# When the second weights of the first two expert tiles are sent, in an attention and mixture-of-experts block on one core

## The chip, the cores and the metric

The kernel runs on one core of a Trainium2 chip. The metric is the device time of one execution in microseconds. The kernel before took 765.93 us as the median of three runs, from 764.69 to 769.72. The profiled execution took 765.39 us, and the span of its instructions 763.7 us.

## The reference, cut to what matters

Two batches of 1024 tokens with 256 features go through causal self attention, cross attention over 77 encoder rows (each with 16 heads of 16), and a mixture of experts, each followed by a residual sum and a layer norm. The experts are what the change touches:

```
router_weights = softmax(x @ rw + rb)            # 8 experts
topw, topi = top_k(router_weights, 2); topw = softmax(topw)
h  = gelu(x @ w1[e] + b1[e])                     # 256 -> 1024
eo = h @ w2[e] + b2[e]                           # 1024 -> 256
out[t] = sum over the two chosen e of topw * eo
```

## The kernel before, in words

Each token is computed only for the two experts that it chose. The 4096 (token, expert) pairs are sorted by expert into at most 39 tiles of 128 rows (NSLOT); a tile has one expert. A tile gathers its 128 token rows from `tokens_scratch` (GpSimd, line 1899), turns them on TensorE (line 1050), multiplies by the first weights w1 (`half_up`, line 849, two halves of 16 matmuls), takes the gelu on ScalarE (line 1177), multiplies by the second weights w2 (`half_down`, line 855), scales on VectorE (lines 1402 and 1404) and puts the rows into `chosen_scratch` (GpSimd, line 1904). Both weights of a tile are 1 MB each. They are loaded into rings: three places for w1 (RING1), two for w2 (RING2).

The first nine tiles (NFIRST) hold tokens of batch 0 only and are worked in the midst of the attention of the last stages, which would otherwise leave TensorE waiting. For that, the string ORDER writes the order of all pieces of work by hand, a letter for a piece; `make_plan` turns it into one list, and every engine walks through that list and does its own part of each piece. So on each engine the order of the instructions is the order of the list, and a piece whose wait isn't over holds up all that the same engine has behind it.

The pieces that matter here:

- `t_weights` (letter B), four times, t = 0 to 3, on ScalarE (lines 1282 to 1291): loads w1 of tile t, from ScalarE's own DMA queue. Each load first reads the tile's expert into a register. From w1 of tile 4 on, line 1312 sends them behind a tile's gelus; from w2 of tile 2 on, line 1306 sends them ahead of them.
- `t_load` (A), on GpSimd: the gather of a tile's tokens.
- `t_turn`, `t_up`, `t_down`, `t_put` (N, U, Y, Z): the tile's work on TensorE, with the waits of lines 1048, 1056 and 1060 for the tokens, w1 and w2.
- `store` and `load` (s, l), on SyncE (lines 2070 and 2092): parts of projected queries go to memory and come back laid out by head.
- `max`, `gather`, `lay` and `score` (m or n, g or h, y, q): the maxima of the scores of a stage are taken (TensorE line 932, VectorE line 1472), split by GpSimd (lines 1974 to 1980), turned (TensorE line 943), sent to memory by SyncE (line 2100) and, when they have landed, back into the rows of the queries (line 2102). The scores (TensorE line 961) wait for that (line 955).

Between the second B and the fourth the list runs: second B, the bias load, one turn of x, the lists of rows, attention of stages 6 and 7, the gathers of tiles 0 to 5, turns of tiles 0 and 1, `t_up` of tile 0, stores and loads of stages 6 and 7, maxima of stage 6, turn of tile 2, third B, maxima, first half of `t_up` of tile 1, fourth B. Then come `t_down` of tile 0, `lay` of stage 6, the second half of `t_up` of tile 1, maxima of stage 7, the scores of stage 6, `t_up` of tile 2 and `t_down` of tile 1.

Of the kernel before, what the change touches and what calls it, by code (L numbers as in the profile page):

```python
# [57 lines left out]
RING1, RING2, RINGX, RINGY = 3, 2, 4, 3  # L58
# [314 lines left out]
def build(nc, x, ctx_in, par, wts, router_w, w1, b1, w2, b2, out):  # L373
# [3 lines left out]
    with stack:  # L377
# [782 lines left out]
        def scalar(act_e):  # L1160
# [8 lines left out]
            def weights2(j):  # L1169
                act_e.dma_start(w2_ring[j % RING2], w2_view[:, bass.ds(expert(j), 1)].rearrange("p e c n -> p (e c) n")).then_inc(  # L1170
                    weights2_in(j)[0], 16)
# [12 lines left out]
            for it in plan:  # L1184
                st = it.st
                bank = work[it.bank]

                if it.kind == "xt" and (it.t % 2 or not it.cross):
                    e.wait_ge(full[it.bank], it.use)
                    act_e.copy(xT[:, :, it.t * P:(it.t + 1) * P],  # L1190
                               bank[:, 0:D].rearrange("p (c n) -> p c n", c=KC)).then_inc(taken[it.bank], 1)

                elif it.kind == "proj":
                    key = st.n, it.at, it.g
                    n = int(st.cross) * 4 + it.at * KC + st.hh
                    bias = b_col[:, n:n + 1]
                    to = part_sb[ring_of[key] // NG][:, 0, it.t:it.t + it.w]
                    e.wait_ge(full[it.bank], it.use)
                    e.wait_ge(taken[columns.bank], columns.use)
                    e.wait_ge(parts_out[ring_of[key]], sent_before[key])  # L1200
                    if st.in_a_hurry:
                        act_e.activation(to, bank[:, 0:it.w], ACT.Identity, bias=bias).then_inc(first_part, 1)
                    else:
                        act_e.activation(to, bank[:, 0:it.w], ACT.Identity, bias=bias)
                        if it.n >= 2:
                            e.wait_ge(*third_ok(rest_after[it.n - 2]))
                        act_e.activation(f_sb[it.n % 2][:, 0:it.w], bank[:, 0:it.w], ACT.Identity,  # L1207
                                         bias=bias).then_inc(taken[it.bank], 1)

                elif it.kind == "rest" and st.in_a_hurry:  # L1210
                    key = st.n, it.at, it.g
                    z = projected[key]
                    e.wait_ge(taken[z.bank], z.use)
                    act_e.copy(part_sb[ring_of[key] // NG][:, 1, it.t:it.t + it.w],
                               f_sb[z.n % 2][:, 0:it.w]).then_inc(second_part, 1)

                elif it.kind == "v":
                    nk, rows = (1, SE) if st.cross else (4, P)
                    e.wait_ge(full[it.bank], it.use)
                    e.wait_ge(const_ok, 1)  # L1220
                    if st.n - 2 in pv_end and st.use > 1 and stage_cross[st.n - 2] == st.cross:
                        buf, use = prob_use(pv_end[st.n - 2], 1)
                        e.wait_ge(prob_taken[buf], use)
                    to = vac[st.slot][0:rows, :, 0:HD] if st.cross else va[st.slot][
                        :, it.t:it.t + nk, :, 0:HD].rearrange("p k h d -> p (k h) d")
                    act_e.copy(to, bank[0:rows, 0:nk * P].rearrange("p (k d) -> p k d", d=HD)).then_inc(taken[it.bank], 1)

                elif it.kind == "lay":
                    e.wait_ge(full[it.bank], it.use)
                    e.wait_ge(negm_out, 16 * it.n)  # L1230
                    act_e.copy(mT[0:3 * HH, :],
                               bank[0:3 * HH, 0:QG // 2].bitcast(bf16)).then_inc(taken[it.bank], 1)

                elif it.kind == "score":
                    rows = SE if st.cross else P
                    w = QG - (0 if st.cross else max(0, it.kb * P - it.g * QG))
                    pair, buf = it.n % 2, it.n % 4

                    e.wait_ge(pair_full[pair], it.n // 2 + 1)

                    if it.n == 2:
                        e.wait_ge(self_apart, 2)
                        e.wait_ge(cross_apart, 2)
                    act_e.activation(pt[buf][0:rows, :, 0:w], st2[pair][0:rows, :, 0:w], ACT.Exp,  # L1244
                                     scale=float(HD) ** -0.5).then_inc(pair_taken[pair], 1)

                elif it.kind == "normalise" and (it.g + it.quad) % 2:
                    buf, use = prob_use(weigh_last[it.n], 1)
                    e.wait_ge(prob_taken[buf], use)
                    if it.n >= 2:  # L1250
                        e.wait_ge(full[divides[it.n - 2].bank], divides[it.n - 2].use)
                    else:
                        e.wait_ge(full[columns.bank], columns.use)
                        for z in ctx_of:
                            e.wait_ge(full[z.bank], z.use)
                    act_e.copy(ot[it.n % 2], o_ps[:, :]).then_inc(o_taken, 1)

                elif it.kind in ("out_turn", "r_turn"):
                    e.wait_ge(full[it.bank], it.use)
                    if it.n >= 2:  # L1260
                        e.wait_ge(*turn_read(it))
                    act_e.copy((onT if it.kind == "out_turn" else rT)[it.n % 2],
                               bank[:, 0:D].rearrange("p (c n) -> p c n", c=KC)).then_inc(taken[it.bank], 1)

                elif it.kind == "out_apply" and it.b == 0:
                    t = it.b * TB + it.t
                    e.wait_ge(scaled, scaled_n[it.cross, it.b, it.t // QT])
                    act_e.activation(res[:, t, :], res[:, t, :], ACT.Identity, scale=rstd[:, t:t + 1],
                                     bias=shift[:, t:t + 1]).then_inc(centred, 1)

                elif it.kind == "w_exp":
                    tl = slice(it.b * TB, (it.b + 1) * TB)
                    e.wait_ge(exps_in, it.b + 1)
                    act_e.activation(ex_l[:, tl, :], lg[:, tl, :], ACT.Exp)
                    act_e.activation(pr[:, tl, :], pr[:, tl, :], ACT.Exp).then_inc(exps_ok, 1)

                elif it.kind == "w_diff":
                    tl = slice(it.b * TB, (it.b + 1) * TB)
                    e.wait_ge(diff_ok, it.b + 1)
                    act_e.activation(wgt[:, 1, tl], dw[:, tl], ACT.Exp).then_inc(second_ok, 1)  # L1280

                elif it.kind == "t_weights":

                    for p in range(2):
                        e.wait_ge(prob_taken[prob_use(last_self, p)[0]], prob_use(last_self, p)[1])
                    e.wait_ge(ej_ok, 1)
                    if it.t >= RING1:
                        e.wait_ge(*up_done(it.t - RING1))
                    weights1(it.t)
                    if it.t < RING2:  # L1290
                        weights2(it.t)

                elif it.kind == "t_turn":
                    e.wait_ge(full[it.bank], it.use)
                    if it.t == 0:
                        for z in find("out_tile", cross=False):
                            e.wait_ge(full[z.bank], z.use)
                    if it.t >= 2:
                        e.wait_ge(*up_done(it.t - 2))
                    act_e.copy(slot_xT[it.t % 2], bank[:, 0:D].rearrange("p (c n) -> p c n", c=KC)).then_inc(taken[it.bank], 1)  # L1300

                elif it.kind == "t_up":
                    if it.t >= 2:
                        e.wait_ge(*down_done(it.t - 2))
                    if it.at == 0 and it.t >= RING2:
                        weights2(it.t)
                    e.wait_ge(full[it.bank], it.use)
                    e.wait_ge(taken[b1_turned.bank], b1_turned.use)
                    half_gelu(it.t, it.at, bank).then_inc(taken[it.bank], 1)

                    if it.at == 1 and 0 < it.t < NFIRST - RING1:
                        weights1(it.t + RING1)
# [885 lines left out]
```

## Time and profile before

| | |
|---|---|
| median of 3 runs | 765.93 us (764.69 to 769.72) |
| profiled execution | 765.39 us, span 763.7 us |
| TensorE matmuls | 720.2 us busy, 94% of the span |
| VectorE, ScalarE, GpSimd | 498.4, 369.6, 286.6 us |
| mean granted TensorE clock | 0.972 of full speed |
| DMA | 140.29 MB, mean 184 GB/s |
| chain that ended last | PE 74%, issue 9%, DVE 7%, DMA 5%, POOL 3%, ACT 1% |

Engines in the rows: PE is TensorE's matmuls, PEld its weight loads, DVE VectorE, ACT ScalarE, POOL GpSimd, SP SyncE; a q behind the name is the engine's sequencer, where DMAs are issued. Times are in microseconds from the start of the span. DMA queues: q10 is the one that ScalarE issues to, q1 SyncE's, q0 GpSimd's.

### The profile page before, as it was taken

How to read it: one execution, taken by the hardware profiler on the slowest of the kernel's cores; microseconds unless marked ns; L12 is line 12 of the kernel's file. 1: busy time of each engine (PE TensorE's matmuls, PEld its weight loads, DVE VectorE, ACT ScalarE, POOL GpSimd, SP SyncE). 2: the span in 40 equal slices, each digit the busy share in tenths (PEclk: the TensorE clock that was granted, in tenths of full speed). 3: DMA queues.
4: the chain of work that ended last, by engine and by line, in shares of the span. 5: the costliest groups of instructions: out<-in, count | busy, mean ns of one | idle time of the engine just before them, and what ended most of it. 6: DMA issues, size and time to landing. Idle time of an engine off the chain costs nothing.

```text
span 763.7 us, 14561 instructions
## 1 busy us (share of the span) xinstructions
PE 720.2 (94%) x4969; PEld 483.5 (63%) x4969; DVE 498.4 (65%) x1376; ACT 369.6 (48%) x749; POOL 286.6 (38%) x558
## 2 busy tenths in 40 slices
PE   6889999999999999999998898999999999999984
PEld 4443434545464455555563676898999999999941
DVE  4679788688766877755766744365656666666436
ACT  3335466665657666677733355433323233332313
POOL 8305522543653553534733223212323322332114
PEclk9999999999999999999986998999999999999997
DMA  8964421243254022315017872686999999999755
GB/s 273 288 146 121 133 78 52 77 126 127 61 151 124 13 60 83 91 46 138 16 58 274 237 223 69 192 272 221 316 337 341 325 340 349 331 335 338 239 180 166
DMA packets 95154, 140.29 MB, mean 184 GB/s; under 512 B 11855, under 2 KB 81077, under 8 KB 92597
## 3 DMA queue, kind: packets, MB, share of 16 engines
q1 hardware_dynamic: 76357, 107.86, 44.8%
q10 hardware_dynamic: 15072, 22.02, 8.8%
q0 software_dynamic: 3648, 9.45, 3.5%
q8 instruction: 41, 0.67, 0.4%
q14 instruction: 36, 0.29, 0.1%
HBM read 110.65 MB, written 28.65 MB: 182 GB/s over the span
## 4 chain that ended last, share of the span: by engine, by line
PE 74%; issue 9%; DVE 7%; DMA 5%; POOL 3%; ACT 1%; DVEq 0%; SPq 0%; ACTq 0%; POOLq 0%
PE out_acc L984 12%; PE score_pair L961 10%; PE work L932 9%; PE score_pair L855 8%; PE work L849 7%; PE work L906 6%; PE work L1008 4%; PE score_pair L849 3%; DVE neg_part_max L1472 3%; PE work L855 3%; PE work L918 2%; PE work L992 2%; PE work L935 2%; DMA arena<-parts_scratch 1%; PE out_acc L849 1%
## 5 line engine op out<-in xcount | busy, mean ns | idle before, releaser
L1472 DVE TENSOR_REDUCE neg_part_max<-work 128x1 f32<-128x512 f32 (+4 forms) x368 | 213.3, 625 | 66.3 <-PE work L935 35.7
L1244 ACT ACTIVATE arena<-score_pair 128x1024 f32<-128x1024 f32 (+2 forms) x224 | 178.8, 839 | 76.6 <-PE score_pair L961 75.4
L932 PE MATMUL work<-arena 96*128 96x77 bf16 (+4 forms) x640 | 118.2, 277 | 10.1 <-ACT arena L1207 2.7
L961 PE MATMUL score_pair<-arena 99*128 99x512 bf16 (+2 forms) x448 | 105.8, 342 | 2.0 <-DMA arena<-negmax_scratch 1.6
L984 PE MATMUL out_acc<-arena 128*32 128x512 f32 (+4 forms) x896 | 104.6, 521 | 0.8 <-DVE arena L1492 0.8
L1904 POOL DMA_INDIRECT chosen_scratch<-arena,scatter_rows x36 | 35.4, 985 | 178.1 <-DVE arena L1404 177.1
L855 PE MATMUL score_pair<-arena 128*128 128x256 f32 x432 | 97.6, 379 | 0.0
L932 PEld LDWEIGHTS work<-arena 96*128 96x128 bf16 x640 | 49.2, 98 | 74.1 <-issue 30.2
L1960 POOL TENSOR_SCALAR_AFFINE_SELECT arena<-arena 128x256 f32<-128x256 f32 x128 | 51.5, 410 | 117.8 <-ACT arena L1244 116.6
L1177 ACT ACTIVATE arena<-work,expert_b_cols 128x128 f32<-128x128 f32 x180 | 51.1, 369 | 84.9 <-PE work L849 79.8
L849 PE MATMUL work<-arena 128*128 128x128 f32 x720 | 88.1, 280 | 0.3 <-issue 0.3
L849 PEld LDWEIGHTS work<-arena 128*128 128x128 f32 x720 | 85.7, 195 | 2.2 <-issue 1.3
L855 PEld LDWEIGHTS score_pair<-arena 128*128 128x128 f32 x432 | 80.1, 190 | 9.8
L1808 DVE STREAM_TRANSPOSE arena<-arena 32x64 f32<-32x64 f32 x304 | 71.6, 235 | 6.2 <-PE score_pair L849 2.1
L961 PEld LDWEIGHTS score_pair<-arena 99*128 99x128 bf16 (+1 forms) x448 | 38.2, 102 | 48.8 <-issue 21.9
L1402 DVE TENSOR_TENSOR arena<-score_pair,arena 128x256 f32<-128x256 f32 x27 | 11.5, 425 | 67.8 <-PE score_pair L855 58.9
L935 PE MATMUL work<-mask_qk,identb 128*128 128x128 bf16 x256 | 48.5, 219 | 0.0
L906 PE MATMUL work<-arena_more,arena 128*128 128x512 f32 x96 | 46.7, 615 | 0.1
L984 PEld LDWEIGHTS out_acc<-arena 128*32 128x32 f32 (+1 forms) x896 | 19.1, 108 | 34.8 <-issue 26.7
L1177 ACT ACTIVATE arena<-score_pair,expert_b_cols 128x128 f32<-128x128 f32 x72 | 20.5, 369 | 38.3 <-PE score_pair L849 37.3
L1008 PE MATMUL work<-arena 128*128 128x256 f32 x128 | 35.4, 411 | 0.6 <-ACT arena L1177 0.5
L849 PEld LDWEIGHTS score_pair<-arena 128*128 128x128 f32 x288 | 34.0, 194 | 0.4
(257 smaller groups left out, 962.5 us busy)
## 6 DMA issues: line engine op xcount, KB each, us to landing
arena<-in_L_xattn_e_w SPq DMA_DIRECT2D x54, 1024.0 KB, 6.2
arena<-parts_scratch SPq DMA_DIRECT2D x24, 768.0 KB, 5.8
arena<-in_L_xattn_e_w ACTq DMA_DIRECT2D x18, 1024.0 KB
parts_scratch<-arena_more SPq DMA_DIRECT2D x24, 384.0 KB, 2.6
parts_scratch<-arena_more SPq DMA_DIRECT2D x24, 256.0 KB, 3.0
parts_scratch<-arena_more SPq DMA_DIRECT2D x24, 128.0 KB, 2.9
residual<-in_x SPq DMA_DIRECT2D x4, 512.0 KB, 7.9
tokens_scratch<-residual SPq DMA_DIRECT2D x2, 1024.0 KB, 4.8
```

The lines of the kernel that those rows point to most:

```text
L849: m = pe.matmul(to[:, q * P:(q + 1) * P], w1_ring[j % RING1][:, c, f * P:(f + 1) * P], slot_xT[j % 2][:, c, :], start=(c == 0), stop=(c == ...
L855: m = pe.matmul(to, act[j % 2][:, c, :], w2_ring[j % RING2][:, c, :], start=(c == 0), stop=(c == FC - 1))
L906: m = pe.matmul(bank[:, 0:it.w], weights[:, c, st.hh * P:(st.hh + 1) * P], src, start=(c == 0), stop=(c == KC - 1))
L932: m = pe.matmul(bank[:, j * it.w:(j + 1) * it.w], qa[st.half(it.g)][0:R_S, h, n0:n0 + P], k, start=True, stop=not it.last)
L935: m = pe.matmul(bank[:, (j + 1) * it.w - P:(j + 1) * it.w], identb[:, :], mask_qk[:, :], start=False, stop=True)
L961: m = pe.matmul(st2[pair][0:rows, j, 0:w], k, qa[st.half(it.g)][0:R_M, h, skip:QG], start=True, stop=True)
L984: m = pe.matmul(o_ps[c * VW:(c + 1) * VW, skip:QG], v, pt[buf][0:rows, j, 0:QG - skip], start=first, stop=last)
L1008: m = pe.matmul(bank[:, 0:D], onT[o.n % 2][:, c, :], (w_cross if it.cross else w_self)[3][:, c, :], start=(c == 0), stop=(c == KC - 1))
L1177: m = act_e.activation(act[j % 2][:, c, :], bank[:, q * P:(q + 1) * P], ACT.Gelu, bias=b1_col[:, bass.ds(ex * FC + c, 1)])
L1244: act_e.activation(pt[buf][0:rows, :, 0:w], st2[pair][0:rows, :, 0:w], ACT.Exp, scale=float(HD) ** -0.5).then_inc(pair_taken[pair], 1)
L1472: dve.tensor_reduce(pm[:, it.at, it.t, it.h0:it.h0 + it.nh], bank[:, 0:it.nh * it.w].rearrange("p (j k) -> p j k", j=it.nh), AX.X, ALU.max ...
L1808: m = dve.transpose(to[b:b + SQUARE, :, a:a + SQUARE], of[a:a + SQUARE, :, b:b + SQUARE])
```

## The change

In the piece `t_weights` the condition and the tile of the second load change. Before, pieces 0 and 1 load w1 and w2 of their own tile. After, pieces 1 and 2 load w1 of their own tile and then w2 of the tile before. All other sends and all waits stay.

```
@@ -1287,8 +1287,9 @@
                     if it.t >= RING1:
                         e.wait_ge(*up_done(it.t - RING1))
                     weights1(it.t)
-                    if it.t < RING2:
-                        weights2(it.t)
+
+                    if 1 <= it.t <= RING2:
+                        weights2(it.t - 1)
 
                 elif it.kind == "t_turn":
                     e.wait_ge(full[it.bank], it.use)
```

The order in which ScalarE sends is then, by pieces (divided by bars): before, w1(0) w2(0) | w1(1) w2(1) | w1(2) | w1(3); after, w1(0) | w1(1) w2(0) | w1(2) w2(1) | w1(3).

## Rows read from the trace of the kernel before

**Rows 1.** The page: its first line, and TensorE's in its part 1.

```profile
span 763.7 us, 14561 instructions
...
PE 720.2 (94%) x4969; PEld 483.5 (63%) x4969; DVE 498.4 (65%) x1376; ACT 369.6 (48%) x749; POOL 286.6 (38%) x558
```

**Rows 2.** Timeline of ScalarE, 396 to 424: start, duration, engine, line, instruction, [idle before].

```profile
408.37 0.39 ACTq L1170 DMA_DIRECT2D arena<-in_L_xattn_e_w  x1
...
411.98 0.37 ACT L1190 COPY arena_more<-work 128x256 f32<-128x256 f32 x1 [2.81 <-PE work L872]
412.66 0.39 ACTq L1166 DMA_DIRECT2D arena<-in_L_xattn_e_w  x1
413.75 0.39 ACTq L1170 DMA_DIRECT2D arena<-in_L_xattn_e_w  x1
```

**Rows 3.** Timeline of ScalarE, 420 to 540.

```profile
433.39 0.39 ACTq L1166 DMA_DIRECT2D arena<-in_L_xattn_e_w  x1
439.36 1.14 ACT L1177 ACTIVATE arena<-work,expert_b_cols 128x128 f32<-128x128 f32 x4 [6.28 <-PE work L849]
440.38 0.39 ACTq L1166 DMA_DIRECT2D arena<-in_L_xattn_e_w  x1
...
446.65 0.39 ACTq L1166 DMA_DIRECT2D arena<-in_L_xattn_e_w  x1
```

**Rows 4.** Timeline of all engines, 436 to 482: TensorE's matmuls.

```profile
438.92 3.70 PE L855 MATMUL work<-arena 128*128 128x256 f32 x16
...
448.14 0.63 PE L961 MATMUL score_pair<-arena 99*77 99x512 bf16 x2
...
449.48 3.84 PE L849 MATMUL work<-arena 128*128 128x128 f32 x32
...
453.16 3.62 PE L855 MATMUL work<-arena 128*128 128x256 f32 x16
...
461.09 0.49 PE L943 MATMUL work<-identb,neg_max_parts 128*24 128x128 bf16 x4 [2.34 <-POOL neg_max_parts L1980]
```

**Rows 5.** DMA queues (packets, MB, share), 411.5 to 414.5, 417 to 421, 447.5 to 449.

```profile
q10 hardware_dynamic: 1021, 1.08, 106.9%
...
q10 hardware_dynamic: 1075, 1.13, 85.4%
q0 software_dynamic: 97, 0.30, 21.5%
...
q10 hardware_dynamic: 51, 0.21, 77.2%
```

**Rows 6.** Timeline of all engines, 402 to 436: the turn of tile 0.

```profile
422.10 0.44 PE L1050 MATMUL work<-ident,arena_more 128*128 128x128 f32 x2 [0.82 <-DVE arena L1458]
```

**Rows 7.** DMA queues, 433 to 437, 437 to 440.5, 444.5 to 445.

```profile
q1 hardware_dynamic: 90, 0.74, 71.5%
...
q10 hardware_dynamic: 259, 1.02, 85.2%
...
q1 hardware_dynamic: 32, 0.02, 13.8%
```

**Rows 8.** Timeline of SyncE's queue, 385 to 470: maxima out and back.

```profile
443.58 0.31 SPq L2100 DMA_DIRECT2D negmax_scratch<-arena_more  x1
445.64 0.24 SPq L2102 DMA_DIRECT2D arena<-negmax_scratch  x1
```

**Rows 9.** Chain of waits, 398.5 to 403: start, duration, what.

```profile
398.90 1.37 DMA negmax_scratch<-arena_more
...
400.29 2.20 DMA arena<-negmax_scratch
```

**Rows 10.** Timeline of GpSimd, 496 to 504: the put of a tile.

```profile
497.10 1.09 POOL L1904 DMA_INDIRECT chosen_scratch<-arena,scatter_rows  x1 [2.69 <-DVE arena L1404]
```

**Rows 11.** DMA queues, 497 to 500.5.

```profile
q10 hardware_dynamic: 968, 1.25, 101.7%
```

**Rows 12.** Stretches: us, busy per engine, granted clock, DMA share, GB/s.

```profile
462.00:468.00 6.00, 6.00 (x19) 4.47 (x20) 1.26 (x6) 3.41 (x4) 1.16 (x2) 0.50 0.20 52
```

More of the change, by code:

```diff
@@ L1289, in scalar @@
                     weights1(it.t)
-                    if it.t < RING2:
-                        weights2(it.t)
+                    if 1 <= it.t <= RING2:
+                        weights2(it.t - 1)
                 elif it.kind == "t_turn":
```

## The prediction

> **What bounds the kernel now.** I read the page first: TensorE is busy for 94% of the span [rows 1], so a late transfer costs time only where TensorE, which works in the written order, stands still for it; and once it does, hardly anything behind it gives the time back. Then I looked in the timeline of ScalarE for the sends that the change touches, in the table of DMA queues (q10 is ScalarE's queue, q1 SyncE's, q0 GpSimd's) for when their bytes move, and in the timeline of TensorE for who waits.
>
> The five DMA rows of the first sends are plain [rows 2]: w2 of tile 0 is sent at 408.37, w1 of tile 1 at 412.66, w2 of tile 1 at 413.75. w1 of tile 2 goes at 433.39 and w1 of tile 3 at 440.38 [rows 3]. The first users are far off: the second matmul of tile 0 starts at 438.92 and that of tile 1 at 453.16 [rows 4]. Neither weight is near its due time before the change.
>
> **The change, step by step.**
>
> *1. The first send loses w2(0).* ScalarE is free for one register load and one issue, 413.75 - 412.66 = 1.09 us [rows 2]. The next of its work on TensorE's way is the copy at 411.98, which waited 2.81 us for TensorE [rows 2]: gain 0. For the same reason w1(1) cannot be sent earlier than 412.66, as it stands behind that copy. So the queue, which moved four loads in one run before, now has a hole between w1(0) and w1(1).
>
> *2. The second send has w2(0) in place of w2(1).* Same count, same bytes. The queue moves 1.08 MB in 3.0 us [rows 5], that is 0.36 MB/us, so one load of 1.05 MB takes 2.9 us. Issue to first bytes is about 1 us, as w1(4), sent at 446.65, has only 51 packets moved by 449 [rows 5], so w1(1) and w2(0) need roughly 413.7 + 5.8 = 419.5 where the four in a row ended between 420 and 421 [rows 5]. w2(0) is due at 438.92: 19 us of cover. The token gathers (q0), which shared the last part of that run [rows 5], come 0.5 to 1 us earlier. Is that worth something? The turn of tile 0 at 422.10 waited for VectorE's line 1458, not for its gather [rows 6]. So 0; the bound for a gain is that whole wait, 0.82 us.
>
> *3. The third send gains w2(1).* It is issued at 433.39 + 1.09 = 434.5. ScalarE stood idle for 6.28 us before its next activation at 439.36 [rows 3], so its own 1.1 us cost nothing; if that cover were gone they would cost 1.1 us. w2(1) is due at 453.16. SyncE's load of 0.74 MB holds the engines till 437 [rows 7], w1(2) moves from 437 to 440.5 [rows 7], w2(1) then to 440.5 + 2.9 = 443.4: 9.8 us of cover. The load of q1 was issued before both and w2(1) stands behind w1(2) in its own queue, so it can't delay those two.
>
> *4. What stands behind w2(1).* w1(3), sent at 440.38, has to follow it: 443.4 + 2.9 = 446.3 in place of about 445. It is for a tile that comes after the second matmul of tile 1 at 453.16 [rows 4], so this alone is harmless. But SyncE sends the maxima of stage 6 out at 443.58 and, once they have landed, back in at 445.64 [rows 8]; the scores at 448.14 need them [rows 4]. In a quiet stretch the same pair took 1.37 and 2.20 us [rows 9]. Here the store took 2.06 us, and its 32 packets moved in 444.5 to 445, when w1(3) was ending [rows 7]: it already waits for what is ahead of it. That such waits are the rule here, the put of line 1904 shows: issued at 497.10, it has not one packet moved by 500.5, while q10 moved 968 from 497 on, alone in that table [rows 10, 11].
>
> So the store lands 1.3 us later. The load before had 448.14 - 445.64 - 2.20 = 0.3 us of room. TensorE then starts the scores 1.0 us late; the maxima that stand between these scores and the matmul at 449.48 keep their order, so there is no further room that I count on. From 449.48 TensorE works without a gap through 453.16; its next idle stretch ends at 461.09 by GpSimd's line 1980 [rows 4], which had itself waited for the put behind tile 1's second matmul: that shifts too. Between 0 (the 24 KB get in among the weights, as some of q0's packets did in the same stretch as q10's [rows 5]) and 3.6 us (second rival), and with the 0.82 us of step 2 as the bound of a gain, I take **+1.0 us**, the value that the store's own row is nearest to.
>
> A rule of the Trainium skill speaks against step 4. It says in "DMA: Bandwidth & Descriptors", section "Queues, rings and completion order", that each DMA engine goes round the queues that have work, packet by packet; by that rule SyncE's 24 KB would slip in between the weights and the sum would be 0 instead of 1.0 us, which is the rival "nothing moves" below. The put at 497.10 [rows 10, 11], which waited for the whole of another queue's backlog, doesn't agree with it.
>
> **Sum.** 0 + 0 + 0 + 1.0 = +1.0 us on the profiled execution of 765.39 us (span 763.7 [rows 1] and 1.7 around it): 766.4. The median of the three runs, 765.93, stands 0.54 above that execution, so the forecast is **766.9 us**.
>
> **The rivals.**
>
> *Second burst.* The return of the maxima would be sent at 445.64 + 1.3 = 446.9, and w1(4) is sent at 446.65 [rows 3]: the order of the two is turned round, which before it was not (445.64 against 446.65). If the load has to wait for w1(4)'s 2.9 us beside its own delay, it lands near 451.7 and TensorE stands still for 3.6 us. Such a gap has a second price: after the 2.34 us without work before 461.09 [rows 4], the granted clock was 0.50 (the lower level, 1.2 GHz) for the six microseconds from 462 [rows 12]. If the clock falls behind the new gap as well, the 7 us of matmuls at 449.48 and 453.16 [rows 4] lose about 6 / 2 = 3 us. This is the case that ends slower: 3.6 to 6.6 us, around 770.5. The point from which it decides is a store that lands after about 446.6. For it: the put at 497.10 [rows 10], and the tie above. Against it: a load's first packets trickle (51 in the 1.5 us from 447.5 [rows 5]), so that a small transfer may get in before them. It passes 1% (7.7 us) only if the clock stays low longer than in that stretch, or if the next gap gets longer too.
>
> *Nothing moves.* The queues mix well enough for 24 KB, as 97 packets of q0 and 1075 of q10 moved in one stretch of 4 us [rows 5], or the hole in step 1 lets everything drain sooner. The time is 765.9, the median of before. For it: w1(3) started slowly before, and it will start at once behind w2(1), so the end of the queue moves by less than I reckon.
>
> *Relief.* The calmer queue between 411.5 and 421 helps: the gathers are early, the wait of 0.82 us at 422.10 [rows 6] goes, and the later work falls so that part of the 6 us at half clock [rows 12] is won back, at most 3 us. Then 0.8 to 3.8 us faster, around 764. Against it: that wait was VectorE's, and the clock has no tie to these loads.
>
> *A weight that comes late.* w2(1) would have to take 18 us from its issue; the three loads sent from 408.37 on were all through by 421, in under 13 [rows 2, 5]. Chance nearly 0.
>
> **How the numbers follow.** Forecast 0.42, second burst 0.26, nothing moves 0.17, relief 0.15. A measurement of this kernel can tell about 1%, 7.7 us, from no change. Of the cases only the far end of the second burst (0.06) goes over that on the slow side, with 0.01 for what I haven't seen; on the fast side the relief case would need twice its bound: 0.03. That leaves 0.90 within 1%. The range: the relief case's middle less a little, 763.3, to the second burst with most of its clock loss, 771.5. It leaves out about 0.1 on each side. The runs of before spread from 764.69 to 769.72, so the ends are not wider than the scatter of single runs makes them.
>
> **What would show it.** Right, in the profile of after: on q10 w1(0), then a hole, then the 4 KB packets of w1(1) (259 for 1.02 MB [rows 7]) and only after 416 the 1 KB packets of w2(0) (1021 for 1.08 MB [rows 5]); w2(1) issued near 434.5 on ScalarE and moved between 440.5 and 443.5; the store of the maxima at 443.6 followed by its return at 446.5 to 447 rather than 445.64; a new short wait of TensorE's line 961 for that return, about 1 us; every later stage of TensorE as much later. Wrong: the return still sent within 2.1 us of the store and the scores at 448.1 (nothing moves); the scores at 451 or later with a granted clock of 0.50 behind them (second burst); the turn of tile 0 before 422.10 (relief). The forecast would be wrong altogether if ScalarE's third send came at another time, as when the maxima of stage 6 shift against it.

## The result, and the profile after

The kernel after took 771.12 us as the median of 20 runs (767.62 to 774.63), the kernel before 764.89 us as the median of 20 runs on the same chip (760.85 to 769.72). The ratio is 1.0082, with a 95% interval of 1.0065 to 1.0099: slower by 6.2 us. That is inside the range of 763.3 to 771.5 and within 1%, but it is not the forecast of 766.9; it is the rival called the second burst. The profiled execution took 772.72 us, 7.33 more than the one before.

The page's first lines, of after [rows 1]:

```profile
span 771.0 us, 14561 instructions
...
PE 722.3 (94%) x4969; PEld 485.4 (63%) x4969; DVE 498.7 (65%) x1376; ACT 369.7 (48%) x749; POOL 286.4 (37%) x558
```

TensorE is busy for only 2.1 us more, in a span that is 7.3 us longer: most of the time went into a wait.

The sends in the timeline of ScalarE, 404 to 450 [rows 2, 3]:

```profile
407.58 0.40 ACTq L1166 DMA_DIRECT2D arena<-in_L_xattn_e_w  x1
413.00 0.40 ACTq L1166 DMA_DIRECT2D arena<-in_L_xattn_e_w  x1
414.11 0.39 ACTq L1170 DMA_DIRECT2D arena<-in_L_xattn_e_w  x1
433.92 0.39 ACTq L1166 DMA_DIRECT2D arena<-in_L_xattn_e_w  x1
435.02 0.39 ACTq L1170 DMA_DIRECT2D arena<-in_L_xattn_e_w  x1
440.89 0.39 ACTq L1166 DMA_DIRECT2D arena<-in_L_xattn_e_w  x1
447.16 0.39 ACTq L1166 DMA_DIRECT2D arena<-in_L_xattn_e_w  x1
```

w1(0) is sent alone, w1(1) and w2(0) together at 413 to 414, w1(2) and w2(1) at 434 to 435, w1(3) and w1(4) behind them. Against the rows of before the sends from 413 on stand 0.3 to 0.5 us later; w1(0), which the change leaves alone, is 0.33 us later already (407.58 against 407.25). The turn of tile 0 was 0.39 us later too, and waited as it did before [rows 6]; timeline of TensorE, 420 to 425:

```profile
422.49 0.44 PE L1050 MATMUL work<-ident,arena_more 128*128 128x128 f32 x2 [0.81 <-DVE arena L1459]
```

So the first two parts of the change cost and gave nothing. Now SyncE's queue, 440 to 460: the maxima of stage 6 go out and, once they have landed, back in [rows 8].

```profile
444.09 0.31 SPq L2101 DMA_DIRECT2D negmax_scratch<-arena_more  x1
448.54 0.24 SPq L2103 DMA_DIRECT2D arena<-negmax_scratch  x1
```

The store took 4.45 us (448.54 - 444.09) where it took 2.06 before. Its return was then issued 1.38 us behind w1(4), where before it went 1.01 us ahead of it. The DMA queues show what each waited for: four stretches, 440.7 to 443.75, 443.75 to 446.25, 446.25 to 448, and 448 to 451.2.

```profile
q10 hardware_dynamic: 958, 1.06, 104.2%
...
q10 hardware_dynamic: 346, 1.00, 106.0%
...
q10 hardware_dynamic: 55, 0.16, 23.3%
q0 software_dynamic: 46, 0.13, 20.3%
q1 hardware_dynamic: 36, 0.02, 4.4%
...
q10 hardware_dynamic: 220, 0.90, 93.0%
```

First come the 1 KB packets of w2(1), then the 4 KB packets of w1(3), and only when that one had but 0.16 MB left did SyncE's (q1) and GpSimd's (q0) packets move at all. In the fourth stretch w1(4) has the engines; the return is issued at 448.54, and by 451.2 none of its packets has moved, while q10 moved 0.90 MB. TensorE, 445 to 470 [rows 4]:

```profile
453.20 1.07 PE L961 MATMUL score_pair<-arena 99*77 99x512 bf16 x2 [4.55 <-DMA arena<-negmax_scratch]
...
455.71 5.04 PE L849 MATMUL work<-arena 128*128 128x128 f32 x32
460.59 3.62 PE L855 MATMUL work<-arena 128*128 128x256 f32 x16
468.52 0.60 PE L943 MATMUL work<-identb,neg_max_parts 128*24 128x128 bf16 x4 [2.34 <-POOL neg_max_parts L1981]
```

The new wait is 4.55 us, and the 32 matmuls of line 849 took 5.04 us in place of 3.84. The granted clock says why; columns are the stretch, each engine's busy time and number of instructions, the clock, the share of the DMA engines and GB/s:

```profile
450.00:452.00 2.00, 0.00 (x0) 0.00 (x0) 0.00 (x0) 0.00 (x0) 1.43 (x7) 0.86 0.81 328
452.00:454.00 2.00, 0.80 (x2) 0.36 (x3) 0.00 (x0) 0.00 (x0) 0.42 (x3) 0.50 0.00 0
454.00:456.00 2.00, 2.00 (x16) 1.42 (x15) 0.79 (x2) 1.59 (x2) 0.00 (x0) 0.50 0.00 0
456.00:458.00 2.00, 2.00 (x11) 2.00 (x11) 1.93 (x6) 0.45 (x1) 0.00 (x0) 0.50 0.36 73
```

During the wait the clock falls from full speed (2.4 GHz) to half (1.2 GHz) and stays there to 458. Before, the whole stretch from 448 to 461 had it at full speed:

```profile
448.00:461.00 13.00, 10.75 (x85) 8.64 (x81) 7.20 (x20) 7.70 (x15) 5.02 (x20) 1.00 0.75 250
```

Behind 460.59 everything stands 7.4 us later, the wait at line 943 is the same 2.34 us, and nothing is given back up to the end.

**A measure for the experiments.** Single executions of one kernel scatter over 7 to 9 us, and the profiled ones differ in where the clock falls ahead of the place in question too: from 386 to 394 it was 0.57 before and after, but 1.00 in those of experiments 4, 5 and 6, though the change and these edits touch only what comes later. So absolute times of two executions are not compared. Besides the medians I use a stretch inside one execution: from the issue of the store of the maxima to the first matmul of tile 1's second product (line 855). It is 453.16 - 443.58 = 9.58 us before and 460.59 - 444.09 = 16.50 after: 6.92 us of the 7.33 lie in it.

### The profile page after: what moved, and what is told of

It is laid out like the page before. It is cut to its first block, busy times and chain, and to the rows that moved or that the text cites. A ratio compares the mean times of both kernels' runs of the same rounds, so it can differ in the third digit from the quotient of the medians.

```text
span 771.0 us, 14561 instructions
## 1 busy us (share of the span) xinstructions
PE 722.3 (94%) x4969; PEld 485.4 (63%) x4969; DVE 498.7 (65%) x1376; ACT 369.7 (48%) x749; POOL 286.4 (37%) x558
## 3 DMA queue, kind: packets, MB, share of 16 engines
q0 software_dynamic: 3648, 9.45, 3.4%
## 4 chain that ended last, share of the span: by engine, by line
PE 74%; issue 9%; DVE 7%; DMA 5%; POOL 3%; ACT 1%; SPq 0%; DVEq 0%; ACTq 0%; POOLq 0%
PE out_acc L984 12%; PE score_pair L961 10%; PE work L932 9%; PE score_pair L855 8%; PE work L849 7%; PE work L906 6%; PE work L1008 4%; DVE neg_part_max L1473 3%; PE score_pair L849 3%; PE work L855 3%; PE work L918 2%; PE work L992 2%; PE work L935 2%; DMA arena<-parts_scratch 1%; PE out_acc L849 1%
## 5 line engine op out<-in xcount | busy, mean ns | idle before, releaser
L961 PE MATMUL score_pair<-arena 99*128 99x512 bf16 (+2 forms) x448 | 106.6, 344 | 6.6 <-DMA arena<-negmax_scratch 6.0
L961 PEld LDWEIGHTS score_pair<-arena 99*128 99x128 bf16 (+1 forms) x448 | 38.4, 103 | 53.3 <-issue 21.9
```

What stands on the lines that cost most here:

```text
L961: m = pe.matmul(st2[pair][0:rows, j, 0:w], k, qa[st.half(it.g)][0:R_M, h, skip:QG], start=True, stop=True)
```

## The experiments

The theory: the cost is two delays in a row, the store behind w2(1) and w1(3) and the return behind w1(4), plus the clock that falls in the gap. The rivals: the later w2(0) costs something too; only one of the two delays decides; the clock doesn't matter.

**1. Only w2(0) moves; w2(1) stays where it was.**

```
-                    if it.t < RING2:
-                        weights2(it.t)
+                    if it.t == 1:
+                        weights2(0)
+                        weights2(1)
```

> Of the change only the move of w2(0) is done: second send w1(1), w2(0), w2(1); third send w1(2) alone. Theory 'backlog' (w2(1) ahead of w1(3) makes SyncE's 24 KB of maxima wait out and back): nothing stands in the queue at 443 that did not before, the store of the maxima takes about 2.1 us, TensorE's line 961 has no long wait at 448, time as before, within 0.2%. Rival 'first sends' (the hole after w1(0) and the later w2(0) cost the time): 5 to 7 us slower.

Measured 766.67 us against 764.5, ratio 1.0036 (1.0006 to 1.0067). The stretch is as before, 9.45 us; the store takes 1.94 and TensorE doesn't wait for its return:

```profile
447.76 0.31 SPq L2101 DMA_DIRECT2D negmax_scratch<-arena_more  x1
449.70 0.24 SPq L2103 DMA_DIRECT2D arena<-negmax_scratch  x1
...
457.21 3.62 PE L855 MATMUL work<-arena 128*128 128x256 f32 x16
```

But the whole was not as before, which was a miss: from the second send to the store this execution takes 33.69 us (414.07 to 447.76), where before took 30.92 (412.66 to 443.58), 2.8 us less. Three loads in one run from 414.07 on keep the queue full for longer, and now the turn of tile 0 does wait for its gather (timeline of TensorE, 410 to 432). The queues of 416.5 to 421 and of 421 to 424 stand below it. The clock was lower as well, 0.88 from 420 to 434 where before had 1.00:

```profile
424.22 0.41 PE L1050 MATMUL work<-ident,arena_more 128*128 128x128 f32 x2 [1.62 <-DMA arena_more<-tokens_scratch,gather_rows]
...
q10 hardware_dynamic: 1083, 1.69, 102.0%
...
q10 hardware_dynamic: 779, 0.78, 81.5%
q0 software_dynamic: 97, 0.27, 26.5%
```

That run of three exists neither before nor after, so this loss isn't one of the change. But the experiment alone doesn't acquit the later w2(0), as its interval lies above 1; for that the next one is needed. What it does show is a small transfer, the gather, that is late behind a run of loads.

**2. Only w2(1) moves.**

```
-                    if it.t < RING2:
-                        weights2(it.t)
+                    if it.t in (0, 2):
+                        weights2(it.t // 2)
```

> Of the change only the move of w2(1) is done: first send w1(0), w2(0); second send w1(1) alone; third send w1(2), w2(1). Theory 'backlog': all of the loss is here, store of the maxima 4 to 4.5 us, wait of line 961 near 4.5 us, 5.5 to 7 us slower than before. Rival 'first sends': as before, within 0.2%.

Measured 769.94 us, ratio 1.0077 (1.0045 to 1.0109): as slow as the whole change. The store takes 3.26 us (446.59 to 449.85), w1(4) is issued at 449.66, again ahead of the return, and TensorE waits. Store and wait are shorter than the 4 to 4.5 and 4.5 us expected:

```profile
452.99 1.07 PE L961 MATMUL score_pair<-arena 99*77 99x512 bf16 x2 [1.82 <-DMA arena<-negmax_scratch]
...
455.49 5.34 PE L849 MATMUL work<-arena 128*128 128x128 f32 x32
460.67 3.62 PE L855 MATMUL work<-arena 128*128 128x256 f32 x16
```

The stretch is 14.08 us, 4.5 more than before, of 5.4 in the profiled execution. Its store was also issued 3.0 us later than before (446.59 against 443.58), with the clock at 0.55 from 438 to 442 where before had 1.00; whether that belongs to the edit or to the execution isn't shown. So the later w2(1) alone makes this loss, with half the store's delay and under half the wait; the clock falls here too. Adding the later w2(0) to it, which is the whole change, costs nothing more that the medians show (1.0082 against 1.0077).

**3. The change, with w1(3) out of the store's way** (sent behind tile 1's gelus, ahead of w1(4)).

```
-                    weights1(it.t)
+                    if it.t < RING1:
+                        weights1(it.t)
...
+                    if it.at == 1 and it.t == 1:
+                        weights1(RING1)
```

> The changed kernel, but w1(3) is sent with w1(4) behind the second gelus of tile 1 (about 447) and not in the fourth send at 440.9. Theory 'backlog': the queue is empty from 443.8 on, the maxima go out in about 1.4 us and are sent back at 445.5, ahead of both loads; no long wait at 448 and the whole loss gone, 5 to 7 us faster than the changed kernel, the same as before or up to 0.7 us better. Rival 'ScalarE's issue' (the 1.1 us that w2(1) adds on ScalarE in the third send is what shifts the work): loss stays.

Measured 765.87 us, ratio 1.0029 (1.0001 to 1.0056): more than half of the loss is gone, though not all of it as expected. The store still takes 3.22 us where 1.4 was expected, since w2(1) itself is ahead of it. TensorE waits only 0.31 us for the return, and yet the clock falls in the stretch from 450 to 453:

```profile
448.15 0.31 PE L932 MATMUL work<-arena 96*128 96x77 bf16 x4 [0.58 <-ACT arena L1302]
448.77 0.62 PE L961 MATMUL score_pair<-arena 99*77 99x512 bf16 x2 [0.31 <-DMA arena<-negmax_scratch]
...
450.10 5.46 PE L849 MATMUL work<-arena 128*128 128x128 f32 x32
...
450.00:453.00 3.00, 3.00 (x22) 3.00 (x19) 2.17 (x6) 1.36 (x2) 1.25 (x6) 0.54 1.02 416
```

The stretch is 12.27 us, 2.7 over before, of which line 849 at the lower clock makes 5.46 - 3.84 = 1.6. Another 0.58 us comes from the edit itself: two sends in a row keep ScalarE from its copy at line 1302, and TensorE waits for that at line 932. That wait stands neither before nor after, but in experiments 6 and 9, which have the same edit.

**4. The change, with w1(4) out of the return's way** (sent behind the first gelus of tile 2).

```
-                    if it.at == 1 and 0 < it.t < NFIRST - RING1:
+                    if it.at == 1 and 1 < it.t < NFIRST - RING1:
...
+                    if it.at == 0 and it.t == 2:
+                        weights1(1 + RING1)
```

> The changed kernel, but w1(4) is sent behind the first gelus of tile 2, after the scores, and not at 447.2. It tells the way out of the maxima from their way back. Theory 'both ways': the store still lands at 448.5 (4.45 us), the way back takes 2.2 us in place of 4.6, line 961 waits about 2.1 us and the granted clock may hold: 3 to 5.5 us faster than the changed kernel, 1 to 3 us slower than before. Rival 'only the way out counts, its last packets linger anyway': wait of line 961 still above 4 us, as slow as the changed kernel.

Measured 768.09 us, ratio 1.0055 (1.0029 to 1.0081): about a third of the loss is gone by the medians, less than the 3 us expected, and the interval touches that of the change. The store takes 4.94 us (441.24 to 446.18), the return 2.35, like the quiet 2.20 [rows 9], against 4.66 after:

```profile
448.53 1.07 PE L961 MATMUL score_pair<-arena 99*77 99x512 bf16 x2 [2.72 <-DMA arena<-negmax_scratch]
...
451.04 5.58 PE L849 MATMUL work<-arena 128*128 128x128 f32 x32
```

So w1(4) costs the return 2.3 us. Both delays are real, and neither alone is the loss. The stretch stays at 15.22 us, as this store was slower than that of after (it was issued while w2(1) was still moving) and the clock fell all the same. That the profiled execution took only 765.04 us, the least of the twelve, doesn't tell against that: it had the clock at 1.00 from 386 to 394.

**5. The change, with TensorE kept at work through the wait.** 80 matmuls whose result is overwritten are put ahead of the wait for the maxima of stage 6.

```
+                    if it.n == 216:
+                        e.wait_ge(pair_taken[pair], use - 1)
+                        for _ in range(80):
+                            pe.matmul(st2[pair][:, 0, 0:P], identb[:, :], identb[:, :], start=True, stop=True)
```

> The changed kernel with 80 extra matmuls of 128x128 (their result is written over) ahead of the first scores of stage 6, where TensorE waits for the maxima; they fill most of the 4.55 us. It prices the clock apart from the wait. Theory 'wait and clock': the wait ends at the same time, but the granted clock stays 1.00 from 448 to 460 and the two runs of matmuls behind take 3.8 and 3.6 us, so 1.5 to 2.5 us are won back against the changed kernel, 768.6 to 769.6. Rival 'the wait is all of it': as slow as the changed kernel, 771.

Measured 765.38 us, ratio 1.0024 (0.9995 to 1.0053), an interval that doesn't touch that of the change. The store is as late as ever (441.86 to 446.28, 4.42 us) and the useful work stands still for the 4.63 us of the filler; only the clock is another:

```profile
446.28 4.63 PE L958 MATMUL score_pair<-identb 128*128 128x128 bf16 x80
450.92 0.63 PE L965 MATMUL score_pair<-arena 99*77 99x512 bf16 x2
...
452.26 3.84 PE L849 MATMUL work<-arena 128*128 128x128 f32 x32
455.93 3.62 PE L855 MATMUL work<-arena 128*128 128x256 f32 x16
...
447.00:450.00 3.00, 3.00 (x58) 3.00 (x55) 0.20 (x1) 0.37 (x1) 2.18 (x11) 1.00 0.75 310
450.00:453.00 3.00, 2.99 (x39) 2.38 (x37) 1.18 (x3) 1.42 (x2) 0.31 (x2) 1.00 0.02 5
```

The stretch is 14.07 us: 2.4 less than after, and 4.5 more than before. So by the two profiled stretches the clock is 2.4 us of the loss and the wait 4.5. The medians give the filler more: 0.0058 of the time, 4.4 us, with intervals of 1.3 and 2.2 us either way. Part of that is the median itself: the twelve runs spread from 762.6 to 772.1, and by the means (766.7 against 764.2 before; 770.9 against 764.9 for the change) 3.6 us are won back. The mean granted clock is 0.977 over the twelve runs and 0.970 over the 20 of the change, which makes some 12 us fewer at the lower level in a run of 765, where this stretch can give about 7. So the clock held in other places too; why isn't shown.

**6. The edit of experiment 3 on the kernel before.**

> The kernel before, but w1(3) is sent with w1(4) behind the second gelus of tile 1. Theory 'backlog': with an empty queue the maxima go out in 1.4 us in place of 2.06, nothing waits for that, the time is as before, within 0.3%. Rival 'any move of these sends costs' (the third kernel of the first series was still 0.3% above the one before): 0.3% slower or more.

Measured 765.34 us against 764.45, ratio 1.0007 (0.9985 to 1.0029), as expected. The store takes 1.41 us (440.37 to 441.78), the same as the quiet 1.37 [rows 9], and it is worth nothing, as TensorE didn't wait for it:

```profile
440.37 0.31 SPq L2103 DMA_DIRECT2D negmax_scratch<-arena_more  x1
441.78 0.24 SPq L2105 DMA_DIRECT2D arena<-negmax_scratch  x1
```

**7. The wait at line 943, which both kernels have.** In the kernel before, the list has GpSimd split the maxima of stage 7 ahead of tile 1's put, not behind it.

```
-    "...na3U2YR2wuZMahyMq2dYR2..."
+    "...na3U2YhR2wuMaZyMq2dYR2..."
```

> The kernel before, but GpSimd splits the maxima of stage 7 ahead of the put of tile 1 (in the written order h stands before Z). The put waits for the second matmul of tile 1 until 458.7, and TensorE stood still for 2.34 us at 461 and then ran 7 us at half clock. Theory 'a piece behind a waiting piece': the gap goes and with it most of the half-clock stretch, 2.3 to 5.5 us faster than before. Rival: TensorE meets the wait for the returned maxima at the scores of stage 7 instead, and wins under 1 us.

Measured 759.67 us, ratio 0.9928 (0.9901 to 0.9955): faster than both kernels. The 2.34 us of idle time are gone, and with them the stretch at half clock behind them [rows 12]:

```profile
458.37 0.39 PE L943 MATMUL work<-identb,neg_max_parts 128*24 128x128 bf16 x4
...
460.48 3.62 PE L855 MATMUL work<-arena 128*128 128x256 f32 x16
...
458.00:464.00 6.00, 6.00 (x37) 5.04 (x38) 2.70 (x13) 4.37 (x5) 3.17 (x3) 1.00 0.48 173
```

**8. The same order in the kernel after.**

> The changed kernel with the order of e7: GpSimd splits the maxima of stage 7 ahead of tile 1's put. My theory: the change's cost lies at the return of the maxima at 444 to 460 us and the gain of the other order lies behind it, at L943, where it takes away a wait of 2.34 us and about 7 us at half clock. The two are separate, so the order gives the changed kernel about the same as it gave the kernel before: 771.1 minus about 5 = 766, and the ratio to the kernel before is 1.001 to 1.003; the wait of L961 stays at 3 to 5 us. Rival: the two share one cost, because with the fall of the clock at 449 the work behind it takes longer and the second wait is covered anyway (less than 2 us gained: 769 to 771). The other rival: the change's loss goes as well (760).

Measured 763.47 us against 763.91, ratio 0.9983 (0.9950 to 1.0016). The gain of the order and the cost of the change stand side by side: the order takes 7.6 us from the changed kernel by the medians and 4.8 from the one before (0.0099 and 0.0072 of the time, which their intervals don't tell apart), and the changed kernel stays 0.55% behind the other with it (0.9983 against 0.9928), with the cost in the same place:

```profile
447.91 1.07 PE L961 MATMUL score_pair<-arena 99*77 99x512 bf16 x2 [4.22 <-DMA arena<-negmax_scratch]
...
448.00:452.00 4.00, 4.00 (x23) 2.98 (x24) 2.05 (x5) 2.04 (x2) 0.58 (x2) 0.50 0.01 4
```

The median was 2.5 us below what I had expected of it; the rivals (769 to 771, or 760) were wrong.

**9. Both edits, 6 and 7, on the kernel before.**

> The kernel before with both edits: the order of e7 and the first weights of tile 3 sent behind tile 1's gelus (e6). The store of the maxima then goes out to a quieter queue (1.4 us for 2.1) and the split follows it. Theory: the edit of e6 alone gave nothing, since L961 hardly waited; with the gap at L943 gone it may give 0 to 0.6 us more: 759 to 760. Rival: first weights that arrive later are missed by tile 3's products: over 1 us slower than e7.

Measured 757.82 us, ratio 0.9903 (0.9869 to 0.9938). It beats both kernels; that it beats experiment 7 isn't shown, since the two intervals overlap for the most part. Its trace answers something that experiment 3 left open. The store takes 1.40 us and TensorE does not wait for the return at all, and still the clock falls, at the scores:

```profile
451.26 0.95 PE L961 MATMUL score_pair<-arena 99*77 99x512 bf16 x2
...
450.00:452.00 2.00, 1.24 (x13) 0.62 (x12) 1.51 (x4) 1.30 (x2) 1.42 (x7) 0.85 0.63 195
452.00:454.00 2.00, 2.00 (x17) 1.49 (x16) 0.86 (x2) 1.99 (x3) 1.42 (x8) 0.50 1.02 418
```

So no wait for the maxima is needed for it. Nor was TensorE less busy ahead of it than in the kernel before, which kept the clock at 1.00: 2.02 of the 3 us from 447.5, against 2.01 of the 3 us from 445, the same place in the work.

| | ratio to before | store | wait of L961 | stretch |
|---|---|---|---|---|
| before | 1 | 2.06 | none | 9.58 |
| after | 1.0082 | 4.45 | 4.55 | 16.50 |
| 1: only w2(0) | 1.0036 | 1.94 | none | 9.45 |
| 2: only w2(1) | 1.0077 | 3.26 | 1.82 | 14.08 |
| 3: w1(3) later | 1.0029 | 3.22 | 0.31 | 12.27 |
| 4: w1(4) later | 1.0055 | 4.94 | 2.72 | 15.22 |
| 5: filler | 1.0024 | 4.42 | 4.63 of filler | 14.07 |
| 6: before, w1(3) later | 1.0007 | 1.41 | none | 10.14 |
| 7: before, split first | 0.9928 | 1.88 | none | 9.46 |
| 8: after, split first | 0.9983 | 4.93 | 4.22 | 15.98 |
| 9: 6 and 7 together | 0.9903 | 1.40 | none | 11.73 |

## Why the prediction had the place right and the sum too small

**Steps 1 to 3 held.** The sends stand where the steps put them (of the first ones there are four, not the five that the prediction speaks of), the queue has its hole (2 packets of q10 from 412 to 414), w2(1) moved from 440.7 to 443.75 (forecast 440.5 to 443.4), no weight came late, and the turn of tile 0 gained nothing. Only the end of w2(0) was put too early, at 419.5: q10 moved at full rate to 420, and had 14 packets left behind 420.5, much as before.

**Step 4, the term of +1.0 us, is the one that failed.** Its chain was right: w1(3) behind w2(1), the store behind both, the return behind the store, TensorE at line 961. But it gave the store too little, and it put two terms at nothing, the return's own delay behind w1(4) and the clock, which stood in the rival. What the rows have in its place is 6.92 us, in three terms:

- The store: 1.3 us more were forecast, 2.39 measured (4.45 - 2.06). I let the end of w1(3) at 446.3 stand for the end of the queue. Its packets did thin out at 446.25, but 55 of q10's were still to come then, and the store's own moved from 446.25 to 447.9. The step took the point at which the queue thins out for the point at which it is empty.
- The return: 2.20 us were forecast, 4.66 measured (453.20 - 448.54). I saw that the order of the return and w1(4) would turn round, and gave that to the second burst. Its point of decision was a store that lands after 446.6; it landed at 448.54. The rival's price of 3.6 us for the gap was near the measured 4.55 (its own terms, 446.9 + 2.20 + 2.9 = 452.0, make it 3.9). Experiment 4 shows that w1(4) is worth 2.3 us of it.
- The clock: not in the sum, 3 us in the rival. Measured 2.37 us: 1.17 between the scores and line 849 (2.51 - 1.34) and 1.20 in line 849 itself. The stretch of experiment 5, where the clock held, is shorter by the same 2.4 us.

2.39 + 2.16 + 2.37 = 6.92, where 2.16 is 4.66 less the 2.50 us that stood before between the return's issue and the scores.

**The choice between the cases.** The measured +6.2 us lies in the band of the second burst, 3.6 to 6.6. That it lies in the range is in part luck: 771.12 is 0.4 us under the upper end, which came from that rival and not from the forecast's case, and the profiled execution, 772.72, is above it. The rival's middle was added up low, too: 765.93 and 3.6 to 6.6 us have it at 771.0, not 770.5. The margin between the forecast and the second burst was a few tenths of a microsecond: a store forecast to be back for its return at 446.9, against w1(4) at 446.65. By my own numbers the return would come second; I took the small case because a load's first packets trickle. They do (5 packets of w1(4) from 448 to 448.25), but the return needs all its packets, and they came last, from 451.2 on. The evidence that I had put beside it, the put that had to wait for the whole backlog [rows 10, 11], was the better guide.

In the return's wait, none of SyncE's packets moved from its issue at 448.54 to 451.2; in experiment 4, where nothing was ahead of it, they moved within 1.3 us of the issue. The Trainium skill says in "DMA: Bandwidth & Descriptors", section "Queues, rings and completion order", that each DMA engine goes round its queues packet by packet. The same section of the Trainium skill lets a packet hold up to 64 descriptors. If the profile's packets are such descriptors, a whole load can be one packet of an engine (1021 over 16 engines are 64). Then a wait for the load in progress does not contradict the rule, and the prediction was too quick to say that the rule makes the sum 0. The row that tells is in experiment 8: the store was issued at 439.11, while w2(1) still moved, and had no packet before 442.5; the rest of w2(1) and three quarters of w1(3) went first (DMA queues, 439.1 to 442.5):

```profile
q10 hardware_dynamic: 715, 1.30, 107.0%
```

On a quiet queue the store's packets start within 0.9 us of the issue (experiment 6: from 441 on, for 440.37), so this one was due at 440.0; the first 4 KB packets of w1(3) moved between 440 and 440.5. A queue that came round after w2(1) would have been served before w1(3), so here the trace doesn't agree with going round. It is not the rule everywhere: from 421 to 424 in experiment 1 packets of q0 moved beside q10's.

**The other rivals.** "Nothing moves" is refuted by the store's 4.45 us. "Relief" is refuted by the turn of tile 0 with its 0.81 us of wait, and by the medians. "A weight that comes late" happened nowhere: in the experiments with later first weights no matmul of lines 849 and 855 waited for one in the stretch.

What stays open is when the clock falls. It fell behind a wait of 4.55 us, behind one of 0.31 us (experiment 3, with TensorE busy for 1.93 of 3 us) and behind none (experiment 9), and in the kernel before, with TensorE busy for 2.01 of 3 us at the same place, it held. So the 2.4 us are measured between two executions, and how often the change pays them isn't shown. Nor is it shown why experiment 5 gained more than its stretch.

## What to carry to other kernels

A large load with time to spare is not free to move: look for the small transfer that is issued next on any other queue, and add the whole backlog to it, down to its last packet. When two small transfers hang on one another and a third load is sent between them, price both delays and not the first alone; and where TensorE waits for them, add what a fall of its clock would cost behind the wait. The list of waits at full length is worth more than the change at hand: moving one letter ahead of another at the next gap gave 0.7%, and both the gap and the half clock behind it were gone.

## What the runs showed of the hardware

- 24 KB out of SyncE's queue took 1.37 to 1.41 us with nothing ahead, 1.88 to 2.06 behind the end of one 1 MB load, 3.22 and 3.26 behind more of one (experiments 3 and 2), and 4.42 to 4.94 where w1(3) had hardly begun.
- The granted clock fell to 0.50 in a wait of 4.55 us, and to 0.54 for the stretch from 450 to 453 behind a wait of only 0.31. With 4.63 us of matmuls without use in the same place it stayed at 1.00. The Trainium skill says in "TensorE: Matmul & The Clock Gate", section "HAM oscillation — how this bites in real kernels", that waits for DMA between groups of matmuls drive the clock up and down; the trace agrees, with 2.4 us lost behind one wait. But the clock fell to 0.50 without any wait for a DMA in experiment 9, too.
- Work without use was thus no loss where TensorE would have stood still anyway: in the one execution profiled, the stretch was 2.4 us shorter with it than without.
